# Two quantising operations of each row tile run on ScalarE instead of VectorE, in a kernel with attention and a quantised linear layer

## The reference, cut to what matters

```python
# X: (4, 1024, 512) float32; 16 query heads, 8 key/value heads of 64
def _L0_attn_ref(X, Wq, Wk, Wv, Wo):
    q, k, v = (X @ Wq), (X @ Wk), (X @ Wv)          # split into heads
    q = q * cos + rotate_half(q) * sin              # the same for k
    att = 50 * tanh(q @ k.T * 256 ** -0.5 / 50)     # causal, softmax
    return (softmax(att) @ v) @ Wo

def _L0_ffn_ref(x, weight, w_scale, bias):
    absmax = jnp.max(jnp.abs(x), axis=-1, keepdims=True)
    in_scale = jnp.maximum(absmax, 1e-7) / 127.0
    q = jnp.clip(jnp.round(x / in_scale), -128, 127).astype(jnp.int8)
    acc = jnp.einsum('bsk,nk->bsn', q, weight, preferred_element_type=jnp.int32)
    return (acc.astype(jnp.float32) * in_scale * w_scale[:, 0] + bias).astype(jnp.float16)

x = _layernorm(x + _L0_attn_ref(x, ...), axis=-1)
x = _layernorm(x + _L0_ffn_ref(x, ...), axis=-1)
```

## Time and profile before

| | us |
|---|---|
| median of three executions | 1497.49 |
| the profiled execution, its own time | 1498.59 |
| its span, first to last instruction | 1496.8 |
| PE busy | 1327.0 (89%) |
| DVE busy | 1094.6 (73%) |
| ACT busy | 847.4 (57%) |
| POOL busy | 379.1 (25%) |
| mean granted clock of TensorE | 0.939 of full |

### The profile page before, as it was taken

How to read it: one execution, slowest core, us unless ns; L and a number is a source line. 1 busy time by engine, 2 the same in 40 slices (tenths; PEclk the granted TensorE clock), 3 DMA queues, 4 the chain that set the end, 5 groups by cost and what they waited for, 6 DMA issues and landing times.

```text
span 1496.8 us, 17694 instructions
## 1 busy us (share of the span) xinstructions
PE 1327.0 (89%) x5824; PEld 964.5 (64%) x5840; DVE 1094.6 (73%) x1367; ACT 847.4 (57%) x952; POOL 379.1 (25%) x448
## 2 busy tenths in 40 slices
PE   6479999888987999998987999989799799999794
PEld 5356777666665777675755677767576577776462
DVE  4368888782687788885477788878357788888485
ACT  4156777761236777864232877676223486779332
POOL 2231111111462111110265112111136311111275
PEclk9889999998998999999899899999899899999896
DMA  7755445474424345537341444445642244343431
GB/s 281 259 194 153 114 112 133 115 213 158 129 61 105 92 115 133 165 84 222 127 140 50 109 118 124 107 146 149 207 136 79 79 115 107 99 108 105 152 108 42
DMA packets 117038, 196.23 MB, mean 131 GB/s; under 512 B 28498, under 2 KB 70484, under 8 KB 112724
## 3 DMA queue, kind: packets, MB, share of 16 engines
q1 hardware_dynamic: 112340, 186.73, 44.1%
q10 hardware_dynamic: 4608, 8.39, 1.5%
HBM read 89.39 MB, written 38.54 MB: 85 GB/s over the span
## 4 chain that ended last, share of the span: by engine, by line
PE 55%; SPq 14%; DVE 11%; DMA 7%; issue 6%; ACT 3%; POOL 3%; DVEq 0%; ACTq 0%; POOLq 0%
PE ps L720 18%; PE ps L694 13%; PE ps L643 13%; SPq L474 8%; PE ps L757 6%; PE ps L665 4%; SPq L487 3%; DMA d_scratch<-sums 2%; DMA rows<-r_scratch 2%; SPq L465 1%; DMA qk<-work_r 1%; ACT probs L888 1%; DVE probs L1138 1%; DVE stats L1159 1%; SPq L490 1%
## 5 line engine op out<-in xcount | busy, mean ns | idle before, releaser
L720 PE MATMUL ps<-prob_hi,v 128*65 128x512 f32 (+3 forms) x1280 | 415.0, 374 | 5.9 <-DVE prob_lo L1077 5.9
L694 PE MATMUL ps<-qk 128*128 128x512 f32 (+1 forms) x1280 | 326.8, 382 | 71.7 <-DMA qk<-work_r 40.3
L888 ACT ACTIVATE probs<-ps 128x1024 f32<-128x1024 f32 x288 | 293.4, 1019 | 148.6 <-PE ps L694 147.2
L1077 DVE TENSOR_TENSOR prob_lo<-probs,prob_hi 128x1024 fp32r<-128x1024 f32 x288 | 355.6, 1235 | 9.9
L1286 POOL TENSOR_SCALAR_AFFINE_SELECT probs<-probs 128x256 f32<-128x256 f32 (+1 forms) x192 | 144.7, 761 | 805.4 <-ACT probs L893 805.4
L694 PEld LDWEIGHTS ps<-qk 128*128 128x128 f32 x1280 | 230.4, 194 | 137.6 <-issue 39.7
L893 ACT ACTIVATE probs<-probs 128x1024 f32<-128x1024 f32 x288 | 305.7, 1061 | 8.8
L1073 DVE CAST prob_hi<-probs 128x1024 fp32r<-128x1024 f32 x288 | 205.9, 715 | 128.4 <-POOL probs L1286 80.1
L643 PE MATMUL ps<-xT,w_ring 128*128 128x512 f32 x1152 | 291.2, 398 | 1.6 <-DVE v L1022 1.5
L643 PEld LDWEIGHTS ps<-xT,w_ring 128*128 128x128 f32 x1152 | 218.9, 192 | 48.5 <-issue 2.2
L720 PE MATMUL ps<-prob_lo,v 128*65 128x512 f32 (+1 forms) x640 | 238.8, 373 | 0.0
(11 more groups left out here) (77 smaller groups left out, 1041.7 us busy)
## 6 DMA issues: line engine op xcount, KB each, us to landing
qk<-work_r SPq DMA_DIRECT2D x256, 128.0 KB, 2.3
qk<-work_r SPq DMA_DIRECT2D x512, 64.0 KB, 2.0
y_scratch<-sums SPq DMA_DIRECT2D x256, 64.0 KB
wo<-wo_scratch SPq DMA_DIRECT2D x8, 2048.0 KB, 8.0
y_raw<-y_scratch SPq DMA_DIRECT2D x32, 512.0 KB, 3.6
w_ring<-w_scratch SPq DMA_DIRECT2D x15, 1024.0 KB, 5.3
x_raw<-X_T SPq DMA_DIRECT2D x16, 512.0 KB, 5.8
x_in<-X SPq DMA_DIRECT2D x32, 256.0 KB, 2.8
```

The costliest lines, as they stand in the source:

```text
L694: mm = nc.tensor.matmul(scores[:, g % 2, col:col + REP * w].rearrange("p (h q) -> p h q", h=REP), qk[:, n % 2, i, 2 + part, keys], qk[:, n ...
L720: mm = nc.tensor.matmul(sums_ps[:, :, GQ - w:GQ], v[:, kt, v0:v0 + width], p[:, g % ring, col:col + REP * w].rearrange("p (h q) -> p h q", ...
L888: nc.scalar.activation(probs[:, g % PRING, :], scores[:, g % 2, :], ACT.Tanh, scale=SCORE_SCALE / SOFTCAP).then_inc(capped, 1)
L1077: nc.vector.tensor_tensor(prob_lo[:, g % PRING, :], probs[:, g % PRING, :], prob_hi[:, g % HRING, :].bitcast(F32), ALU.subtract).then_inc( ...
```

## The change

`round_up` and `round_down` are two new columns that hold ROUND and -ROUND, set by POOL at the start. DVE's `quantise` becomes `find_scale`, which ends with the inverse. ACT gets the two other operations as its own `quantise(t-1)`, behind `norm1(t-1)` and `norm2(t-3)`. The second still waits for `turn_q` of the tile before. DVE's next `find_scale` now waits for ACT's first operation of the tile before (`q_big_done`) and no longer for `q_done`.

```diff
+            def quantise(b, t):                        # on ScalarE
+                act.wait_ge(inv_done, rows_upto(b, t))
+                if (b, t) == (0, 0):
+                    act.wait_ge(rounds_set, 2)
+                nc.scalar.activation(q_big, z[:, t % 2, :], ACT.Identity, bias=round_up[:, 0:1],
+                                     scale=inv_scale[:, 0:1]).then_inc(q_big_done, 1)
+                act.wait_ge(q_big_done, rows_upto(b, t))
+                if t >= 1:
+                    act.wait_ge(q_turned, rows_upto(b, t - 1))
+                nc.scalar.activation(q16[:, :], q_big, ACT.Identity, bias=round_down[:, 0:1]).then_inc(q_done, 1)
...
                     norm1(b, t - 1)
                     if t >= 3:
                         norm2(b, t - 3)
+                    quantise(b, t - 1)
...
                 norm2(b, NT - 3)
+                quantise(b, NT - 1)
                 store(b, NT - 3)
...
-            def quantise(b, t):                        # on VectorE
+            def find_scale(b, t):
                 dve.wait_ge(z_done, rows_upto(b, t))
                 if t >= 1:
-                    dve.wait_ge(q_done, rows_upto(b, t - 1))
+                    dve.wait_ge(q_big_done, rows_upto(b, t - 1))
...
                 nc.vector.reciprocal(inv_scale[:, :], in_scale[:, t % 4:t % 4 + 1]).then_inc(inv_done, 1)
-                dve.wait_ge(inv_done, rows_upto(b, t))
-                nc.vector.tensor_scalar(q_big, z[:, t % 2, :], inv_scale[:, 0:1], ROUND, ALU.mult,
-                                        ALU.add).then_inc(q_big_done, 1)
-                dve.wait_ge(q_big_done, rows_upto(b, t))
-                if t >= 1:
-                    dve.wait_ge(q_turned, rows_upto(b, t - 1))
-                nc.vector.tensor_scalar(q16[:, :], q_big, ROUND, None, ALU.subtract).then_inc(q_done, 1)
...
+            nc.gpsimd.memset(round_up[:, :], ROUND).then_inc(rounds_set, 1)
+            nc.gpsimd.memset(round_down[:, :], -ROUND).then_inc(rounds_set, 1)
```

More of the change, by code:

```diff
@@ L176, in attention_block @@
         minus_half = sb("minus_half", [P, 1])
+        round_up = sb("round_up", [P, 1])
+        round_down = sb("round_down", [P, 1])
         eps = sb("eps", [P, 1])
@@ L213, in attention_block @@
         const_zero = sem("const_zero")
+        rounds_set = sem("rounds_set")
         const_made = sem("const_made")
@@ L1246, in _ @@
                         shift_by(b, t - 3, 1, rstd2, shift2)
-                    quantise(b, t - 1)
+                    find_scale(b, t - 1)
                     residual1(b, t)
@@ L1255, in _ @@
                 shift_by(b, NT - 3, 1, rstd2, shift2)
-                quantise(b, NT - 1)
+                find_scale(b, NT - 1)
                 rescale(b, NT - 2)
```

## The result

The changed kernel takes 1472.68 us (median of 4 runs, 1470.67 to 1473.56) against 1497.10 before (4 runs, 1494.16 to 1499.59): the ratio is 0.9836, 95% interval 0.9815 to 0.9857. The profiled execution took 1470.67 us, its span is 1468.9 us. Against the profiled execution of before (1498.59) that is 27.9 us less, where 26.4 was forecast.

The account below looks back on a forecast made before the run. DVE, stretched by lockout with POOL, was taken to pace the tails over PE. Terms of 13.7, 6.4, 3.7 and 2.6 us made 26.4, from 1498.59 to 1472.2, median 1471; own range 1466 to 1476, eight in ten 1465 to 1484.

Parts of the forecast that it names:

- What bounds it: Tails from tile 4: DVE sets the pace at 8.79 us per tile; with 2.71 gone, PE's 7.59 would.
- Why the two operations were long: Quantisation on DVE: two-port mode and POOL lock each other out, stretching 0.485 and 0.426 us to 2.71 together.
- The price on ACT: Quantisation pair moved to ACT: 0.80 us each, 1.66 for the pair, bounds 1.25 and 2.17.
- The second chain: Output projection, from `turn_q` through `keep_q`, `y_hi`, `y_lo`: ends at 6.4 to 6.6 us, wanted at 7.59.
- Waits for `y_lo`: PE in front of `project_out`, all four tails: 13.7 of 14.0 us of waiting go.
- The clock: One tile's `project_out` per tail ran at a lower clock behind a stall; without stalls 4 x 1.6 = 6.4 us go.
- Behind the last `project_out` of batches 1 to 3: End of the first three tails: DVE came late to a finished acc; 1.4, 1.4 and 0.9, together 3.7 us go.
- The last batch: End of the last tail: 1.8 us before `residual1(7)` and 0.86 before the last but one `rescale` go, 2.6.
- Handed on whole: Between tails: what the first three tails gain passes whole through the next attention stage, whose loads shift or were issued earlier.
- The clock drops: Rival, in the tails: lower clock levels stay, 6.4 us is not gained, 1477.5 us; chance 0.13.
- the first tails count: Against the rival that their gain is lost at the next attention stage, leaving 9.0 us, 1488.5; chance 0.07.
- ACT's loop: Slower rival, tile to tile: costs once the pair exceeds 2.5 us, at 4.5 us gives 1513; chance 0.04.

## Why the prediction was right, step by step

- *What bounds it.* DVE set the pace of the tails from tile 5, in the last batch from tile 4, by 8.79 against 7.59. Shown three ways: with DVE relieved PE's starts are 7.59 apart, with DVE filled to 8.50 they are 8.50 apart, and with 1.42 us of filler, which fits into the gap, nothing changes. The rest that I left to DVE, 6.08 us, still held the idle 0.30 for POOL; without gaps it is 8.50 - 2.81 = 5.7. Between those two lengths the rule "DVE's length against PE's" was too simple: with the second operation moved, and with both in the form with a sum, DVE was shorter than PE and a tile still took 7.7 to 8.0 us, by the loop through POOL.
- *Why the two operations were long.* The rule on the lockout from the page "SBUF — State Buffer" of the Trainium skill (Who interferes with whom) carried the whole forecast; the runs agree (746 and 686 ns without the double mode, 1.34 us with it beside `y_lo` and 1.41 beside `f`), and on ACT the two do not vary by more than 6 ns. The prediction named POOL's partner for the first operation alone.
- *The price on ACT.* I took 0.80 for each and 1.66 for the pair; it is 0.816 + 0.723, 1.57 from start to end. The second operation is 93 ns shorter than the first. So 0.92 us is to spare and not 0.8; the fillers on ACT agree within 0.1 (at least 0.85 by the one, 0.84 by the other).
- *The second chain.* The output projection was to close with 1.0 to 1.2 us to spare. The low part was to end 6.6 us after the start of `project_out` and ended at 6.75 to 6.98, later in each tile, since its loop through POOL and DVE is 7.70 us long. It closed with 0.83, 0.72 and 0.05 us, the last by luck: the prediction had no row on this loop.
- *Waits for `y_lo`.* 13.7 us were to go, 13.7 went (14.0 to 0.3).
- *The clock.* No drop in the four places, as forecast. But this term and the waits are not two sums that add, and 4 x 1.6 = 6.4 was too much for the drops alone. With the change in the last batch alone two tails had the waits and no drop, and were only 0.3 to 0.4 us shorter for it; their waits for `y_lo` were 1.2 to 1.3 us longer. The drop in the last tile of the first batch cost about 1.1 (59.4 us from the spreading of tile 5 on, against 58.3). The total of both terms holds, since what a drop took there the next wait gave back. The tie "a stall brings the drop" is looser than I used it, too: before, the clock fell behind the wait for the rows of tile 4 in the second batch, after, it did not. That gave about 1.5 us by chance and is why the second tail gained 7.3 where the terms give 5.6.
- *Behind the last `project_out` of batches 1 to 3.* DVE now waits 1.28 us in front of `rescale(6)` for PE, where it came 1.4 late. The first and the third tail gained 6.4 and 5.6; the terms of the sum give 6.3 and 5.6. Counted from the spreading of tile 5, behind the place where the clock fell by chance, the four tails gained 6.4, 5.7, 5.7 and 9.6 us.
- *The last batch.* `residual1(7)` starts 0.03 us after the matmuls end (1449.39 + 0.40 against 1449.82) where it started 1.8 after. From there to the end it is 19.1 us where it was 20.4: 1.3 less, of which 0.86 had been named. The sum for this tail, 9.4, is 0.4 above the forecast 9.0.
- *Handed on whole.* True in the mean, with 0.8 us of loss in sum. But it hides pieces of up to 2.3 us in one stretch, most of which are waits for DMAs that land earlier or later. The own range of 1466 to 1476 allowed for it; the agreement of 27.9 with 26.4 is partly luck, since the median fell by 24.4.
- *The rivals.* The clock drops did not stay; no steady tile waits in `turn_q`; the first tails count; ACT's loop exists and starts to cost where I read it, but lies 0.9 us away. Its price was too low in my working: 1513 at a pair of 4.5 us, while a pair of about 4.1 already gives 1519.5.

## What to carry to other kernels

When a DVE operation has one length in some tiles of a kernel and three times that in the tiles that matter, look at what POOL does beside it before counting DVE's capacity, and see whether it ends just behind an operation of POOL. Here another engine and another form both ended the stretching; another order was not tried. Compare two engines by their length per tile in the stage, not by their shares of the span, and then follow the moved work around its loop and write down the time to spare, for each loop: here 0.85 us more on ACT cost almost nothing, and 2.5 us more turned a gain of 24 us into a loss of 22. A wait shows at whatever its late engine feeds next, so a group of waits that has gone does not yet say that the late engine has.

## What the hardware showed that I had not expected

- A DVE operation that also accumulates its sum was faster here than the plain one: 0.746 and 0.686 us and an own read of 0.08, against 1.34 and 1.41. It had the same length whatever POOL did beside it.
- The lockout seems to cost POOL too: in the steady tiles of the last tail the 128x512 `f` took 1.47 us before, and 1.28 or 1.29 in the kernel after and in the one that accumulates. The longer `y_lo` did not change (2.35 to 2.40 us in all of them), but `f` follows `y_lo` at once, while a DVE operation is still held up, and it is then the one that is longer by 0.19 us.
- On ACT the operation with one column operand took 0.723 us, that with two 0.816, at the same width. The first also writes bfloat16, so no run here separates the two reasons.
- The granted clock need not fall behind a stall of 2 us (2.00 us and then 1.00), nor is it the same from one execution to another at the same place, and it can fall behind 1.14 us (the start at 783.82 in the earlier trace rows, and 0.51 in the window from 786 to 788). Where DVE set the pace, a drop inside tile 6 cost 0.3 to 0.4 us and not the 1.6 by which it slows the tile.
